# Layer 0's biases in a recurrence of two layers: from TensorE's products to a bias column in ScalarE's gates

## The reference, cut to what matters

```python
x: (32, 128, 128)    h_first = cond_1024: (32, 128)
# layer 0, for each t; b has 4 * 128 numbers
a = x[:, t] @ Wx + b + h @ Wh
i, f, o = sigmoid(a[:, :128]), sigmoid(a[:, 128:256]), sigmoid(a[:, 256:384])
g = tanh(a[:, 384:])
c = f * c + i * g
h = o * tanh(c)
# layer 1, for each t, on x1 = x + h of layer 0
m = concat(x1[:, t], h1) @ weight + bias
g1 = sigmoid(m[:, :128] + 1.0)
h1 = g1 * h1 + (1 - g1) * tanh(m[:, 128:])
```

## Time and profile before

| | |
|---|---|
| median of 3 runs | 228.70 us (228.32 to 232.32) |
| the profiled execution's own time | 228.34 us |
| its span, first to last instruction | 226.2 us |
| mean granted TensorE clock | 0.998 of 2.4 GHz |
| busy: PE / PEld / DVE / ACT / POOL | 221.1 / 206.6 / 198.8 / 134.1 / 3.7 us |
| instructions: PE / DVE / ACT | 4850 / 1555 / 903 |

### The profile page before, as it was taken

The page is one execution under the profiler, slowest core; times in us unless marked ns, Lnnn a source line. Parts: engine busy times, 40 slices in busy tenths (PEclk is TensorE's granted clock), DMA queues, the critical chain, the costliest instruction groups (busy, mean ns, idle before and its releaser), DMA issues.

```text
span 226.2 us, 12499 instructions
## 1 busy us (share of the span) xinstructions
PE 221.1 (98%) x4850; PEld 206.6 (91%) x4850; DVE 198.8 (88%) x1555; ACT 134.1 (59%) x903; POOL 3.7 (2%) x12
## 2 busy tenths in 40 slices
PE   7999999999999999999999999999999999999994
PEld 5899999999999999999999999999999999999883
DVE  4889989899899898998998998989989989899895
ACT  3655666656566666665566566665666666656652
POOL 2400000000000000000000000000000000000000
PEclk9999999999999999999999999999999999999999
DMA  6000001010010001000010001101001000000000
GB/s 186 26 17 26 16 26 49 14 29 26 20 45 26 24 20 49 26 16 26 28 39 26 26 14 29 49 14 28 26 21 46 26 26 16 26 16 16 14 14 14
DMA packets 12006, 6.70 MB, mean 30 GB/s; under 512 B 1447, under 2 KB 11693, under 8 KB 11949
## 3 DMA queue, kind: packets, MB, share of 16 engines
q1 hardware_dynamic: 11376, 5.33, 8.4%
q10 hardware_dynamic: 572, 0.59, 0.7%
HBM read 3.82 MB, written 2.10 MB: 26 GB/s over the span
## 4 chain that ended last, share of the span: by engine, by line
DVE 79%; ACT 11%; issue 4%; PE 3%; DMA 1%; ACTq 0%
DVE cell_bank L574 13%; ACT act_bank L492 11%; DVE hT L581 8%; DVE pair L595 7%; DVE x1T L623 7%; DVE acts L603 7%; DVE scan_add L568 7%; DVE h_high L582 6%; DVE u_rest L609 6%; DVE outT L631 6%; DVE pair L597 6%; DVE h_low L588 6%; DMA xT<-in_x_dram 1%; PE a L291 1%; PE a L283 0%
## 5 line engine op out<-in xcount | busy, mean ns | idle before, releaser
L265 PE MATMUL gate_f<-hT,wh_raw 128*128 128x32 f32 x254 | 47.0, 267 | 0.3 <-DVE hT L581 0.2
L265 PEld LDWEIGHTS gate_f<-hT,wh_raw 128*128 128x128 f32 x254 | 37.8, 188 | 9.8 <-DVE hT L581 8.1
L473 ACT ACTIVATE gate_f<-gate_f 128x32 f32<-128x32 f32 x127 | 23.1, 182 | 34.2 <-PE gate_f L265 34.2
L492 ACT ACTIVATE act_bank<-cell_bank 128x32 f32<-128x32 f32 x128 | 23.3, 182 | 33.3 <-DVE cell_bank L574 33.2
L581 DVE TENSOR_TENSOR hT<-out_gate,act_bank 128x32 f32<-128x32 f32 x128 | 23.9, 187 | 21.0 <-ACT act_bank L492 21.0
L498 ACT ACTIVATE acts<-a 128x64 f32<-128x64 f32 x128 | 28.6, 223 | 17.8 <-PE a L291 4.6
L574 DVE TENSOR_TENSOR_SCAN cell_bank<-act_bank,scan_add 128x64 f32<-128x64 f32 x128 | 38.0, 297 | 0.1
L283 PE MATMUL a<-h_high,w1x_scaled 128*128 128x32 f16 x256 | 35.4, 177 | 0.2
L283 PE MATMUL a<-h_high,w1x_third 128*128 128x32 f16 x256 | 35.4, 177 | 0.0
L283 PE MATMUL a<-h_high,w1x_rest 128*128 128x32 f16 x256 | 35.4, 176 | 0.0
L285 PE MATMUL a<-h_low,w1x_fp 128*128 128x32 f16 x256 | 35.4, 176 | 0.0
(11 more groups left out here) (114 smaller groups left out, 1071.9 us busy)
## 6 DMA issues: line engine op xcount, KB each, us to landing
xT<-in_x_dram SPq DMA_DIRECT2D x45, 64.0 KB, 2.0
out_dram<-outT SPq DMA_DIRECT2D x32, 64.0 KB, 1.6
wx_s<-in_L_cond_Wx_dram SPq DMA_DIRECT2D x1, 256.0 KB, 2.9
wh_raw<-in_L_cond_Wh_dram ACTq DMA_DIRECT2D x1, 256.0 KB, 3.3
w_raw<-in_L_cond_weight_dram ACTq DMA_DIRECT2D x1, 256.0 KB, 3.5
xT<-in_x_dram ACTq DMA_DIRECT2D x1, 64.0 KB, 3.3
bias_rows<-in_biases_dram ACTq DMA_DIRECT2D x1, 3.0 KB
condT<-in_cond_dram SPq DMA_DIRECT2D x1, 16.0 KB, 3.2
```

The lines of the kernel that those rows point to most:

```text
L265: nc.tensor.matmul(gate_step(GATE_F, j), wh_raw[:, GATE_F * P:(GATE_F + 1) * P], hT[:, (j - 1) % RING, :], start=False, stop=True, skip_gr ...
L473: return nc.scalar.activation(out, gate_step(q, j), func)
L492: nc.scalar.activation(tanh_c[:, :], cell[:, :, 1], ACT.Tanh).then_inc(tanh_c_ready, 1)
```

## The change

Layer 0's biases come as a second input, `bias_cols`: the same numbers, laid out as 128 partitions x 4 gates, loaded by one more DMA that SP issues behind that of `condT` (each partition gets 16 bytes). ScalarE's four gate instructions name the column of their gate as their bias operand, a 128 x 1 tile in SBUF in place of the number 0.0. `bias0` and its 67 products are gone from TensorE. ScalarE waits for the new load ahead of its wait for `wh_raw`. TensorE's waits for `pick_ready` and `bias_ready` move from the start to just ahead of the first `bias1`, in step 1. Layer 1's biases stay as they are.

```diff
+        bias_cols = sb("bias_cols", [P, NG])
...
+        b_in, b_cols_in = sem("b_in"), sem("b_cols_in")
...
             sp.dma_start(condT[:, :], h_first).then_inc(cond_in, 16)
+            sp.dma_start(bias_cols[:, :], b_cols).then_inc(b_cols_in, 16)
...
-            def bias0(q, first, steps=GS):
-                k = (first - BEGIN[q]) % GS
-                nc.tensor.matmul(gate_banks[q][:, k * N:(k + steps) * N], bias_lhs[:, :],
-                                 pick[:, q:q + 1].to_broadcast([P, steps * N]),
-                                 start=False, stop=False, skip_group_check=True)
...
             pe.wait_ge(wx_in, 16)
-            pe.wait_ge(pick_ready, 1)
-            pe.wait_ge(bias_ready, 1)
             project0(GATE_I, 0, 3)
-            bias0(GATE_I, 0, 3)
             pe.wait_ge(x_in[1], 16)
             project0(GATE_G, 0, 5)
-            bias0(GATE_G, 0, 5)
...
             project0(GATE_O, 0, 7)
-            bias0(GATE_O, 0, 7)
             first_state(GATE_O, o_summed)
...
                             project1(1, 0, 0, 0)
+                            pe.wait_ge(pick_ready, 1)
+                            pe.wait_ge(bias_ready, 1)
                             bias1(0, 0)
...
                         layer1_low(r, l)
-                    if k in (0, 2, 4, 6):
-                        bias0((GATE_F, GATE_I, GATE_G, GATE_O)[k // 2], a, BODY - a if ends else GS)
...
             nc.scalar.activation(blank[:, 0:1], blank[:, 0:1], ACT.Sigmoid)
+            act.wait_ge(b_cols_in, 16)
             act.wait_ge(wh_in, 16)
...
             def gate(out, q, j, func):
-                return nc.scalar.activation(out, gate_step(q, j), func)
+                return nc.scalar.activation(out, gate_step(q, j), func, bias=bias_cols[:, q:q + 1])
...
+        "bias_cols": _by_gate(_np.asarray(inputs["L0_cond_b"]).reshape(1, -1)).reshape(NG, d).T,
```

More of the change, by code:

```diff
@@ L38, with two_layer_recurrence @@
 WARM = 15
-def two_layer_recurrence(nc, xt, h_first, wx, wh, b, w1, out_t):
+def two_layer_recurrence(nc, xt, h_first, wx, wh, b, b_cols, w1, out_t):
     xt_h = xt.rearrange("d (g c) -> g d c", g=HALVES)
@@ L115, in two_layer_recurrence @@
         cond_in, wx_in, wh_in, w1_in = sem("cond_in"), sem("wx_in"), sem("wh_in"), sem("w1_in")
-        b_in = sem("b_in")
+        b_in, b_cols_in = sem("b_in"), sem("b_cols_in")
         out_free = [sem(f"out_free{i}") for i in range(SLOTS)]
@@ L678, in _ @@
             add_layer1(BODY - 1, T)
-_INS = ["x", "cond_1024", "L0_cond_Wx", "L0_cond_Wh", "biases", "L1_cond_weight"]
+_INS = ["x", "cond_1024", "L0_cond_Wx", "L0_cond_Wh", "biases", "bias_cols", "L1_cond_weight"]
 def kernel(**inputs):
```

## The result

| | before | after |
|---|---|---|
| median | 228.43 us (6 executions, 228.19 to 232.32) | 262.49 us (6 executions, 259.15 to 286.97) |
| ratio, with its 95% interval | | 1.142 (1.138 to 1.145) |
| span of the profiled execution | 226.2 us | 257.0 us |
| its own time | 228.34 us | 259.16 us |
| first hT starts at | 7.15 | 7.45 |

The change makes the kernel 14% slower. The executions of the changed kernel differ in their granted clock: two took 259.2 us at a mean of 0.98, one 262.0 at 0.954 and one 263.0 at 0.946. The profiled one is one of the two of 259.2 us.

A forecast was written before the change was run, and what follows sets the result against it. The bound was taken as a ring closing once per time step, with three ScalarE gates in series, not TensorE. 36.2 - 0.5 + 0.4 = +36.1 us on 228.3 gave 264.4, stated as 264.5 us; range 238 to 270.

The forecast's parts named there:

- the main one: Each gate's bias read on ScalarE is serial and costs one trip to SBUF, 75 to 105 ns: 257 to 269 us, chance 0.63.
- a smaller serial price: Rival: a read costs a third to three quarters of a trip to SBUF, 240 to 257 us; chance 0.06.
- The ring: One loop step, hT to next hT, 1.68 us: the scan waits for serial gates f, g, i; forecast +0.285 us.
- The price of a read: ScalarE's gate instructions: each bias read adds 95 ns, serial, to duration and distance of starts; three per step, 36.2 us.
- What goes off, -0.5: The step into every eighth, 0.03 us longer for VectorE's late layer 1 pair, loses that excess: 15 steps, -0.5 us.
- worth nothing: Removing TensorE's 67 bias products gains nothing, since they hide behind the wait for the state.
- What I had called nothing: gate o: Gate o on ScalarE starts 0.285 us later but ends ahead of the tanh, so it costs nothing.
- The start: ScalarE's wait for the bias load, landing at 5.3, delays the first scan and tanh: +0.4 us, bounds 0 and about 1.
- The clock: Rival: TensorE's clock falls to 1.2 GHz in the loop, an estimated 0.1 us per step, 277 us; chance 0.04.

## Why the prediction was right, and where not

The prediction was 264.5 us, and the median is 262.5; the profiled execution took 259.2. Its ground is shown: the gates are in series on the ring, the operand read is serial, and the loop pays three of them. That the number came so close is luck, since the sum is made of errors that nearly cancel. By the prediction's own branches the price of a read, 0.209/3 = 0.070 us, lies below the 75 to 105 ns of the main one and in the rival "a smaller serial price", which had a chance of 0.06 and 240 to 257 us. The time came out above those 257 only by what the prediction had at nothing: gate o and the clock.

- **The ring.** Right: the scan starts 0.04 behind the end of gate i, before and after, and gate f stays at 0.69 after hT.
- **The price of a read.** Mis-sized: the term was 95 ns, from a whole trip to SBUF. Measured are +80 ns in gate f's duration, and +0.07 in the distances. A step pays by the medians 0.074 + 0.069 in the distances and 0.072 in gate i's duration, 0.215, of which 0.209 was seen, and not 0.285. The 123 steps from step 5 on cost 25.7 us so, and steps 1 to 4 only 0.4 together: 26.1 us and not 36.2. The sum took each of the 127 steps at the full price. The second operand, at 0.09, is what the estimate had; the first one is cheaper. The 93 ns of the Trainium skill, "ScalarE: Activation LUTs", section "What ACT_TABLE_LOAD costs", agree with the second operand in these runs (85 to 93) and are above the first in three of four durations (72 to 83, gate o 94) and in the distances (69 to 75).
- **What goes off, -0.5.** The number came, from another cause. VectorE's slack covers its late path, but with the products in place the step into k = 7 is 1.915 us, since the product of gate o delays the next forget product. It needs the removal as well. So "worth nothing" was wrong by 0.03 us in one step of eight, once gate o is late.
- **What I had called nothing: gate o.** I looked at the tanh, which it doesn't delay, and wrote that TensorE's waits move along with the scan. The wait of gate o's projections for `o_ready` doesn't: gate o's end came 0.31 later in a step that grew by 0.21. That is +1.8 us into k = 0.
- **The start.** +0.4 predicted, +0.30 measured, as the sum of +0.57 for the wait and about -0.3 for the missing products, each good to some 0.1 us. So here too two terms offset each other, and the products are not worth nothing in the start. The 2 us of the Trainium skill, "DMA: Bandwidth & Descriptors", section "Anatomy of one DMA — SWDGE (gpsimd) path", for the fixed part of a transfer (this load is issued by SP, not on that path) would have had it there at 4.1 (an estimate); the trace has it at 5.1, 3.0 us after its issue at 2.12.
- **The clock.** It was a rival with a chance of 0.04, placed in the loop. It came in the start, where I hadn't looked, and cost 3.1 us in the profiled execution; the two at a mean of 0.954 and 0.946 were 3 and 4 us longer still. I priced the products as hidden time. I did not ask what TensorE's clock does in the start when they are gone.

So 36.1 was expected in all and 30.8 was measured in the profiled execution: 10.1 too much for the reads and 0.1 for the start, 1.8 (gate o) and 3.1 (clock) not foreseen.

## What to carry to other kernels

Ask of each operand whether it sits in the instruction or is read from memory: here the same number, a zero, cost 0.07 to 0.08 us more in SBUF than in the instruction, in a ring that paid it three times per step. The broadcast product, on an engine that waited anyway, was the cheaper place for this bias. When work is taken from TensorE as "hidden", look at its granted clock in every stretch afterwards, and in more than one execution. When an instruction gets slower, follow every semaphore that it raises, not only the one on the main ring.

## What the runs showed of the hardware

- A bias read from SBUF adds 72 to 94 ns to the duration of an ACTIVATE of 128 x 32 (gate f 182 to 262, gate o 203 to 297) and 69 to 75 ns to its distance from the next (0.112 to 0.186 and 0.101 to 0.170 us); a scale read as well adds 85 to 90 ns more to the duration (gate f 352) and 90 to 93 to the distance (0.277 and 0.263).
- Behind a gate f with such an operand, gates without one followed each other at 0.077 us, where the distance was 0.101 before: the 0.10 isn't the floor.
- TensorE's clock went to its lower level and back in the middle of loops that do the same from step to step (for 3.4 us at 178, for 34 us at 177), in some kernels and executions and not in others. What in the work decides it stays open. In the start the idle time ahead of the first forget product does not decide it (the clock fell at 0.30 us and held at 0.38), and one of four executions with only the operands added, all products in place, had a mean of 0.976. The kernel before had a mean of 0.994 or more in every execution that ran beside these.
